# A recurrent cell's gate sums on two halves of the partitions, and the work around its steps rescheduled

## The reference

```python
x = x + deformable_conv3x3(group_norm(x))        # offsets, masks, bilinear gather
t = tokens(x)                                    # 4 sequences of 256 tokens, 64 channels
t = t + attention_block(layer_norm(t))           # 8 heads of 32, gated GELU FFN, two norms
t = t + recurrent_cell(layer_norm(t))            # over the 256 tokens, in order
```

```python
def step(h, c):
    i = sigmoid(xi_t + h @ V_i)
    g = tanh(xg_t + h @ V_c)
    o = sigmoid(xo_t + h @ V_o)
    c = h * c + i * g          # h stands where a forget gate would
    h = o * tanh(c)
```

## Time and profile before

| | us |
|---|---|
| median of 3 runs | 424.03 (423.84 to 425.36) |
| profiled execution, time | 425.57 |
| profiled execution, span | 423.8 |
| TensorE busy (matmul) | 399.5 (94%) |
| VectorE, ScalarE, GpSimd busy | 240.2, 262.9, 59.3 |

### The profile page before, as it was taken

How to read it: one execution, slowest core, us unless ns; L and a number is a source line. 1 busy time by engine, 2 the same in 40 slices (tenths; PEclk the granted TensorE clock), 3 DMA queues, 4 the chain that set the end, 5 groups by cost and what they waited for, 6 DMA issues and landing times.

```text
span 423.8 us, 14792 instructions
## 1 busy us (share of the span) xinstructions
PE 399.5 (94%) x5669; PEld 215.5 (51%) x5669; DVE 240.2 (57%) x1161; ACT 262.9 (62%) x1127; POOL 59.3 (14%) x131
## 2 busy tenths in 40 slices
PE   8999998888999899999999999999899999999996
PEld 2555553545455455545555554555455545554332
DVE  2477745154565566656565656665566656565443
ACT  1676643563786587568748865876587568744443
POOL 6000004001111111012111102111111012110000
PEclk9999998999999999999999999999999999999999
DMA  7000000000000000000000000000000000000000
GB/s 243 0 2 2 2 2 0 0 2 2 3 3 2 4 6 2 4 2 5 5 2 5 4 2 4 5 3 3 2 6 3 2 2 7 3 3 5 2 2 5
DMA packets 2244, 3.78 MB, mean 9 GB/s; under 512 B 1277, under 2 KB 1726, under 8 KB 2174
## 3 DMA queue, kind: packets, MB, share of 16 engines
q1 hardware_dynamic: 1872, 2.32, 1.8%
q10 hardware_dynamic: 302, 0.52, 0.4%
HBM read 2.57 MB, written 0.26 MB: 7 GB/s over the span
## 4 chain that ended last, share of the span: by engine, by line
PE 69%; DVE 12%; ACT 12%; issue 5%; DMA 1%; POOL 1%; DVEq 0%
PE bank L349 20%; PE bank L620 15%; PE bank L478 7%; DVE bank L1036 5%; PE bank L416 5%; PE bank L404 5%; PE bank L489 4%; DVE H L1046 4%; ACT bank L760 4%; PE bank L506 3%; ACT bank L753 3%; PE bank L377 2%; ACT E L734 2%; ACT QB L726 2%; PE bank L518 1%
## 5 line engine op out<-in xcount | busy, mean ns | idle before, releaser
L349 PE MATMUL bank<-FB 128*128 128x512 bf16 (+3 forms) x677 | 184.4, 369 | 1.2 <-DVE FB L786 1.2
L620 PEld LDWEIGHTS bank<-H,VW 128*32 128x32 f32 x3072 | 53.0, 109 | 92.9 <-DVE H L1046 88.1
L620 PE MATMUL bank<-H,VW 128*32 128x4 f32 x3072 | 75.6, 179 | 12.6 <-DVE H L1046 5.6
L1036 DVE TENSOR_TENSOR_SCAN bank<-bank,SU 64x12 f32<-64x12 f32 x256 | 48.7, 190 | 64.9 <-ACT bank L753 62.2
L753 ACT ACTIVATE bank<-bank 64x8 f32<-64x8 f32 x256 | 37.9, 148 | 73.1 <-PE bank L620 72.1
L1046 DVE SCALAR_TENSOR_TENSOR H<-TO,bank 64x4 f32<-64x4 f32 x256 | 40.9, 160 | 49.2 <-ACT bank L760 47.4
L349 PEld LDWEIGHTS bank<-FB 128*128 128x128 bf16 x677 | 50.9, 99 | 31.4 <-issue 5.7
L760 ACT ACTIVATE bank<-bank 64x4 f32<-64x4 f32 x256 | 38.8, 152 | 17.6 <-DVE bank L1036 2.9
L757 ACT ACTIVATE TO<-bank 64x4 f32<-64x4 f32 x256 | 44.1, 172 | 6.3
L1030 DVE SCALAR_TENSOR_TENSOR SU<-H,bank 64x4 f32<-64x4 f32 x256 | 41.4, 162 | 9.0
L333 POOL TENSOR_SCALAR E<-E,rinv 128x256 f32<-128x256 f32 x56 | 27.0, 481 | 139.5 <-DVE rinv L909 139.5
(11 more groups left out here) (117 smaller groups left out, 341.1 us busy)
## 6 DMA issues: line engine op xcount, KB each, us to landing
AW<-in_attn_w SPq DMA_DIRECT2D x1, 768.5 KB, 8.1
DW<-in_dcn_w SPq DMA_DIRECT2D x1, 576.0 KB, 6.7
X<-in_x_fm SPq DMA_DIRECT2D x1, 256.0 KB, 3.3
X<-in_x_fm ACTq DMA_DIRECT2D x1, 256.0 KB, 5.2
out_dram<-OUT SPq DMA_DIRECT2D x8, 32.0 KB, 1.4
CW<-in_conv_w SPq DMA_DIRECT2D x1, 243.5 KB, 4.2
VEC<-in_vecs SPq DMA_DIRECT2D x1, 160.0 KB, 8.0
K<-in_consts ACTq DMA_DIRECT2D x1, 154.0 KB, 3.6
```

What stands on the lines that cost most here:

```text
L349: nc.tensor.matmul(idle[:, 0:n], FB[:, 0:P], FB[:, 0:n], start=True, stop=True)
L620: mm = nc.tensor.matmul(gate_out(m, gate, r, slice(B * s, B * (s + 1))), VW[:, gate, r], H[:, (STEPS * m + s - 1) % RING, :], start=False, ...
L1036: nc.vector.tensor_tensor_scan(CS.rearrange("p b q -> p (b q)"), GT.rearrange("p b q -> p (b q)"), SU[:].rearrange("p b q -> p (b q)"), 0. ...
```

## The change

- The candidate gate's sums go to partitions 64 to 127 of the cell bank, beside i's on 0 to 63; the o gate's sums move to partitions 0 to 63 of the bank b_cs (columns by tile parity), and its preload waits for the last o tanh of the tile before. Sums and preload use start=True for every gate. The sums' operands are cut to rows 0 to 63 (before, 128 rows, of which 64 were zeros).
- The gates' tanh covers 128 partitions and writes each result twice into a tile IG in SBUF. u goes to IG too. The scan takes its multipliers from partitions 0 to 63 of IG and its addends from 64 to 127, one element shifted, over 15 elements.
- LEAD becomes 33: a tile's offset o now falls in cell step s = o - 1. CELL_INPUT and CELL_READY, one later in offsets, stay in their steps; all else comes a step earlier. NARROW comes at 24. The FFN's norms are spread over more steps, and some pieces change between `beside_gates` and `beside_tanh`.
- NS_STEP is 730 instead of 820, NS_TABLE 620 instead of 900. Filler columns in a GELU table step go from 2944 to 2176, in an exp table step from 2560 to 2048, in a step with scores from 640 to 384, in one with turning and weighing from 512 to 384; plain steps keep 1536. In the step where preload and scores meet there are none, nor in the one of a leaving tile with scores.

```diff
-NARROW = 25
+NARROW = 24
 NARROWED = 26
-STATS = (22, 26, 28)
-AGGR = (23, 26, 28)
-CENTRED = (24, 27)
-SCALED = (24, 28, 29)
-CELL_INPUT = 30
-CELL_READY = 31
-LEAD = 32
+STATS = (22, 27, 29)
+AGGR = (23, 27, 30)
+CENTRED = (25, 28)
+SCALED = (26, 29, 31)
+CELL_INPUT = 31
+CELL_READY = 32
+LEAD = 33
...
-NS_STEP = 820
+NS_STEP = 730
-NS_TABLE = 900
+NS_TABLE = 620
...
-        SU = sb("SU", [C, B, 3])
+        IG = sb("IG", [P, B, 4])
...
-        CS = b_cs[C:P, 0:3 * B].rearrange("p (b q) -> p b q", q=3)
-        TC = b_cs[C:P, 3 * B:4 * B]
-        GT = b_cs[0:C, 0:3 * B].rearrange("p (b q) -> p b q", q=3)
+        CS = b_cs[C:P, 0:4 * B].rearrange("p (b q) -> p b q", q=4)
+        TC = b_cs[C:P, 4 * B:5 * B]
+        ig = IG[:].rearrange("p b q -> p (b q)")
...
-            half, place = ((0, 0), (0, P), (C, 0))[gate]
-            return b_cell[m % 2][half + rows.start:half + rows.stop, place + cols.start:place + cols.stop]
+            half, place = ((0, 0), (C, 0), (0, P * (m % 2)))[gate]
+            return (b_cell[m % 2], b_cell[m % 2], b_cs)[gate][half + rows.start:half + rows.stop,
+                                                              place + cols.start:place + cols.stop]
...
                 for gate in range(3):
+                    if gate == 2 and m >= 1:
+                        pe.wait_ge(o_gate, STEPS * m)
                     nc.tensor.matmul(gate_out(m, gate, slice(0, C), slice(0, P)), UW[:, gate, :],
-                                     XT[:, m, :, :].rearrange("p s b -> p (s b)"), start=(gate != 1), stop=True,
+                                     XT[:, m, :, :].rearrange("p s b -> p (s b)"), start=True, stop=True,
...
-                    mm = nc.tensor.matmul(gate_out(m, gate, r, slice(B * s, B * (s + 1))), VW[:, gate, r],
-                                          H[:, (STEPS * m + s - 1) % RING, :], start=False, stop=True,
+                    mm = nc.tensor.matmul(gate_out(m, gate, r, slice(B * s, B * (s + 1))), VW[0:C, gate, r],
+                                          H[0:C, (STEPS * m + s - 1) % RING, :], start=False, stop=True,
...
-                    nc.scalar.activation(GT[:, :, 1:3].rearrange("p b g -> p g b"),
-                                         b_cell[m % 2][0:C, 0:2 * P].rearrange("p (g s b) -> p g s b", g=2, b=B)[:, :, s, :],
+                    nc.scalar.activation(IG[:, :, 0:3:2],
+                                         b_cell[m % 2][:, B * s:B * (s + 1), None].to_broadcast([P, B, 2]),
                                          ACT.Tanh).then_inc(gates, 1)
...
-                    nc.vector.tensor_tensor_scan(CS.rearrange("p b q -> p (b q)"),
-                                                 GT.rearrange("p b q -> p (b q)"),
-                                                 SU[:].rearrange("p b q -> p (b q)"), 0.0,
+                    nc.vector.tensor_tensor_scan(CS.rearrange("p b q -> p (b q)")[:, 0:4 * B - 1],
+                                                 ig[0:C, 1:4 * B], ig[C:P, 0:4 * B - 1], 0.0,
                                                  op0=ALU.mult, op1=ALU.add).then_inc(cell, 1)
```

More of the change, by code:

```diff
@@ L293, in _ @@
             nc.gpsimd.memset(XT[:], 1.0).then_inc(zeroed, 1)
-            nc.gpsimd.memset(SU[:], 1.0).then_inc(zeroed, 1)
+            nc.gpsimd.memset(IG[:, :, 0:3], 0.0).then_inc(zeroed, 1)
+            nc.gpsimd.memset(IG[:, :, 3], 1.0).then_inc(zeroed, 1)
             nc.gpsimd.memset(YF[:], 0.0).then_inc(zeroed, 1)
@@ L443, in _ @@
             pe.wait_ge(ld_aw, 16)
-            pe.wait_ge(zeroed, 9)
+            pe.wait_ge(zeroed, 10)
             pe.wait_ge(yf_done, 2)
@@ L701, in _ @@
                                ).then_inc(at_sb, 1)
-            act.wait_ge(zeroed, 9)
+            act.wait_ge(zeroed, 10)
             act.wait_ge(t0_mm, 2)
@@ L801, in _ @@
             nc.vector.tensor_tensor(gvar[:], gmv[:, :, 1:2], gsq[:], ALU.subtract).then_inc(gn_var, 1)
-            dve.wait_ge(zeroed, 9)
+            dve.wait_ge(zeroed, 10)
             dve.wait_ge(gn_rs, 1)
@@ L956, in beside_gates @@
                         nc.vector.memset(CS, 0.0).then_inc(cs_zero, 1)
-                        nc.vector.memset(GT[:, :, 0], 0.0).then_inc(cs_zero, 1)
                     if o in EXP_AT:
@@ L979, in beside_gates @@
                                                 GE[:].rearrange("p j q -> p (j q)"), ALU.mult).then_inc(ff_done, 1)
[L980 to L983, removed]
                     if o == STATS[1]:
@@ L986, in beside_gates @@
                         norm_stats(m, 1, R2[:])
+                    if o == AGGR[2]:
+                        norm_aggr(m, 2)
                     if o == CENTRED[1]:
@@ L990, in beside_gates @@
                         scale(m, 1, T1[:, m, :], R2[:], TB[:, m, :]).then_inc(t1_done, 1)
-                    if o == STATS[2]:
-                        dve.wait_ge(t1_done, m + 1)
-                        norm_stats(m, 2, T1[:, m, :])
+                    if o == SCALED[2]:
+                        norm_apply(m, 2, LN3[:], T1[:, m, :]).then_inc(ln3_done, 1)
                     if o == CELL_READY:
@@ L1017, in beside_tanh @@
                         norm_aggr(m, 1)
[L1018 to L1021, removed]
+                    if o == NARROWED:
+                        dve.wait_ge(ff_mm, m + 1)
+                        dve.wait_ge(x1_done, m + 1)
+                        nc.vector.tensor_tensor(R2[:], b_t[:, 0:C], X1[:], ALU.add).then_inc(r_done, 1)
+                    if o == STATS[2]:
+                        dve.wait_ge(t1_done, m + 1)
+                        norm_stats(m, 2, T1[:, m, :])
             for g in EVERY:
@@ L1028, in _ @@
                     else:
-                        dve.wait_ge(cs_zero, 2)
-                    nc.vector.scalar_tensor_tensor(out=SU[:, :, 2], in0=H[0:C, (g - 1) % RING, :], scalar=0.5,
+                        dve.wait_ge(cs_zero, 1)
+                    nc.vector.scalar_tensor_tensor(out=IG[C:P, :, 1], in0=H[0:C, (g - 1) % RING, :], scalar=0.5,
                                                    in1=CS[:, :, 2], op0=ALU.mult, op1=ALU.mult).then_inc(u_done, 1)
```

## The result

The changed kernel takes 430.9 us (430.74 to 431.89, 4 runs) where the kernel before takes 424.49 beside it: 1.0155 times as long, 95% interval 1.0129 to 1.0181. It is slower by 6.4 us, clear of no change, where 4.9 us of gain were forecast, and it lies outside the range of 413.5 to 428.

What follows compares the result with a forecast made beforehand. The recurrence, a closed chain taking 312 of 424 us, was taken to bound the kernel. Links -3.8, crowded steps -1.25 and prologue +0.2 gave -4.9 us, so 419.2 us on the median; range 413.5 to 428.

Steps and rivals of the forecast that it cites:

- The third bound: Gate sums: if four busy column blocks cost 24 ns, the gain is 27 ns a step instead of 51.
- The link sum: Plain step's chain: sums -51, gates' tanh +27, scan +8 ns, taken as -15, for a step of 1.129 us.
- (a): GELU table load, 7 tiles: step 1.90 us, 1.87 before; the 0.29 of late sums in the next step vanishes.
- (b): Exp table load, 6 tiles: the step behind it 0.18 us over a plain one, with QB copies and LN3; 0.49 before.
- (c): Preload and first scores meet in one step: the next sums come 0.51 us late, 6 times.
- (d): Norm steps: one operation each; only the product FF waits for GELU and may cost 0.03 us.
- (e): Output: L901 and L1003 in one step put it 0.16 us over a plain step, 6 times.
- (f): QB steps: 75 ns over plain; after an exp, ScalarE 24 and VectorE 14 ns; 33 ns of late sums go.
- (1): Rival for the whole kernel: the column blocks do not help the sums, link +35 ns, 427.7 us; chance 0.16.
- (2): Rival for the whole kernel: the sums gain only 27 ns, link +8, 423.1 us, no tellable change; chance 0.18.
- (3): Rival: link at -31 ns and K = 64 shortens the way through the array, 412 to 416 us; chance 0.13.
- (4): Rival: TensorE's clock falls in steps with 384 or no filler columns; one stretch a tile gives 430 us; chance 0.07.

Runs made afterwards that it cites:

- e1: Changed kernel with the offsets, norms and filler of the kernel before, so only the cell's new layout and tanh remain: 435.75 us, 1.0266 of the kernel before.
- e2: Changed kernel with the cell of the kernel before, so only the new schedule and filler remain: 419.86 us, 0.9887 of the kernel before.
- e3: Kernel before with only fewer filler columns, NS_STEP 730 and NS_TABLE 620: 418.14 us, 0.9848 of the kernel before.
- e4: Kernel before with only the scan's addends (SU) moved to partitions 64 to 127: 434.33 us, 1.0233 of the kernel before.
- e8: Kernel before with only the scan's multipliers (GT) in SBUF, partitions 0 to 63, instead of PSUM: 427.96 us, 1.0087 of the kernel before.
- e7: Kernel before with NS_STEP 730, NS_TABLE 440, LEAD 32 and FFN and norm pieces spread one to a step: 415.09 us, 0.9785 of the kernel before.

## Why the prediction was wrong

**The step that failed** is the one that took VectorE's overlap for granted: "After an exp, ScalarE's last read and VectorE's L901 may hold back another 24 and 14 ns". The 14 ns come out only if the new scan may start some 80 ns ahead of the end of L901, as it does in the trace of before (75 ns in the median, 79 at most), and that was carried over to a scan with other operands without a reason. What the runs show in its place is a scan that starts 31 ns behind that end: 112 ns in each of six steps a tile (4.7 us in seven tiles). By the same hold the step with the product is about 0.1 longer than forecast, the one with the heads' copy about 0.05, the one with the output 0.08, the one with R2 (offset 26), now behind the scan and in front of H, 0.07, and the even steps some 15 ns. The cell alone costs 11.5 us (e1), of which the links are 1.5; the remaining 10 are nearly all held steps (9.7 by the trace). No rival had it. The trace of before held the clue: in the crowded step of the earlier trace rows the scan starts behind L946's end, and I put that down to two operations in one step.

**The size of the miss** is 11.3 us, 6.4 slower where 4.9 faster was forecast. 5.4 of it are the links, below. The rest is in the crowded steps: they come to 24.8 us over 255 plain ones of 1.150, where 18.0 was forecast. (The forecast also counted 19.2 of such time in the kernel before, where the trace has 20.1.)

**Gate sums.** The starts came as read from L506 (0.07), so the reading of the earlier trace rows was right. By the rule of the Trainium skill that the prediction cites ("TensorE: Matmul & The Clock Gate", Part 3) the new place would have given nothing. The trace does not agree: eight matmuls on the same rows start within 73 ns, and the tanh came 33 ns earlier. The term was mis-sized all the same: 33 ns, not 51. The third bound (27) was the nearer one; why the release comes 18 ns later behind the last start stays open.

**Tanh and scan** were forecast at +27 and +8 and came at +30 and +10. The link sum of +6 against -15 is 5.4 us of the miss. Its range was given as -31 to +23, but the bounds stated for its terms give -27 and not -31 at the lower end.

The crowded steps, one by one:

- **(a)** 1.908 against a forecast 1.90, and the late sums behind it are gone.
- **(b)** Forecast 0.18 over a plain step, came 0.11. The forecast had LN3 behind the scan (0.04 of it), and the two QB copies hold the tanh by 0.11 and not 0.14.
- **(c)** The sums are 0.513 late, as forecast (0.514); a held scan adds 0.04, which makes 0.554 over a plain step. In e2 the sums alone are 0.556 late.
- **(d)** The narrow matmuls, which stand in front of the next sums (0.10 late), and not the norms made offset 26 long before. With the product a step earlier they do so at offset 25 (e2: 1.257), which I had not seen. In the changed kernel the held product step hides them.
- **(e)** 0.24 instead of 0.16, held once more.
- **(f)** ScalarE's 24 ns came as forecast, and the 33 ns of late sums went, as e3 shows too.
- **Prologue:** +0.2 was forecast. The first H is written at 108.3 us, as in the four runs that keep the prologue of before (e1, e3, e4, e8: 108.2 to 108.6), so no effect can be told. The 109.4 of the earlier trace rows are of an execution that took 1.5 us more than the median.

The rivals: (1) gives nearly the measured sign and size, 427.7, but by a mechanism that did not occur. (2) has the link nearly right, +8 where +6 came; its 423.1 lacks the held steps. (3) and (4) did not occur.

## What to carry to other kernels

Before an operand is moved to other partitions on VectorE, look at what is issued in front of and behind its reader: in these traces an overlap of some 75 to 90 ns was there only while start partitions agreed, and without it a short operation behind a long one cost 0.11 us each time. Filler that follows the critical matmuls is free only as long as it ends before the next step's: here two constants gave 6.2 us, and a new cell layout cost 11.5. And take a change of several parts apart before judging it; this one held a gain of 4.4 us inside a loss of 6.4.

## What the runs showed that was not expected

- ScalarE overlaps too, in the new layout: the o gate's tanh starts 74 ns behind the start of the gates' tanh, which lasts 177, where before it started 24 ns behind its end. The prediction had it waiting behind the other. Both now read PSUM from partition 0 and write SBUF. Writing SBUF is not enough: in e8 both do, the o gate's is read from partition 64, and its tanh still starts 25 ns behind the other's end. What decides was not tried. It is off the chain here.
- The gates' tanh starts 237 ns behind the last start of its sums when they lie on four column blocks and the o gate's follow them, and 219 ns when they lie on two and start last.
- With the smaller filler the clock row still reads nine in all of the recurrence: with 640 columns cut to 384 and 2944 to 2176, and in e7 with 1664.
